# Stage A of a graph kernel: x loaded block by block into two places that TensorE reads, in place of one bulk load and a staging copy

## What is computed

```python
ones = jnp.ones((src.shape[0],), feats.dtype)
deg_out = jnp.clip(jax.ops.segment_sum(ones, src, num_segments=n), 1.0)
deg_in = jnp.clip(jax.ops.segment_sum(ones, dst, num_segments=n), 1.0)
h = feats * jax.lax.rsqrt(deg_out)[:, None]
m = jax.ops.segment_sum(h[src], dst, num_segments=n) * jax.lax.rsqrt(deg_in)[:, None]
gc = m @ W_gc + b_gc
x = gc + (feats @ W_res + b_res)
core = _moe_ff(x, Wg, bg, w1, b1, w2, b2)      # top-2 of 64 experts, gelu between two matmuls
y = x + core                                    # then batch norm over nodes, + feats, layer norm
```

## Time and profile before

| | |
|---|---|
| median of 3 runs | 1657.07 us |
| lowest, highest | 1651.96, 1659.29 us |
| the profiled execution | 1655.46 us |
| its span in the profile | 1653.6 us |
| mean granted clock of TensorE | 0.957 of full |
| TensorE matmuls busy | 1483.0 us, 90% |
| TensorE weight loads busy | 1253.0 us, 76% |
| VectorE busy | 1096.2 us, 66% |
| ScalarE busy | 697.4 us, 42% |
| GpSimd busy | 469.6 us, 28% |
| DMA on SyncE's and ScalarE's main queue | 150.59 MB, 27.8% of 16 engines' span |
| largest lines on the chain that ended last | TensorE L1070 32%, L1176 13%, L1185 12%, L1058 9%, L974 4% |

### The profile page before, as it was taken

How to read it: one execution, slowest core, us unless ns; L and a number is a source line. 1 busy time by engine, 2 the same in 40 slices (tenths; PEclk the granted TensorE clock), 3 DMA queues, 4 the chain that set the end, 5 groups by cost and what they waited for, 6 DMA issues and landing times.

```text
span 1653.6 us, 42138 instructions
## 1 busy us (share of the span) xinstructions
PE 1483.0 (90%) x11682; PEld 1253.0 (76%) x11683; DVE 1096.2 (66%) x2604; ACT 697.4 (42%) x1610; POOL 469.6 (28%) x442
## 2 busy tenths in 40 slices
PE   5988858999999999999999997699999999999662
PEld 4866747877777787777777786688888888888562
DVE  6976898787788788788778775344444444444377
ACT  1647765443434344434443442233333333333257
POOL 4356100112112112111111212455555555555100
PEclk9998979999999999999999998799999999999785
DMA  9212110101101101101101022786667856763594
GB/s 295 80 61 60 58 37 10 43 14 39 51 13 38 51 13 38 51 13 38 37 27 38 20 71 71 230 271 224 214 218 247 270 178 226 251 215 97 186 301 151
DMA packets 146095, 188.11 MB, mean 114 GB/s; under 512 B 16117, under 2 KB 114200, under 8 KB 145763
## 3 DMA queue, kind: packets, MB, share of 16 engines
q1 hardware_dynamic: 126034, 150.59, 27.8%
q0 software_dynamic: 18144, 35.99, 6.8%
q10 hardware_dynamic: 1872, 1.02, 0.2%
HBM read 141.42 MB, written 51.21 MB: 116 GB/s over the span
## 4 chain that ended last, share of the span: by engine, by line
PE 76%; DVE 6%; issue 5%; ACT 4%; DMA 2%; another core or an unknown queue 2%; DVEq 2%; SPq 1%; POOL 0%; ACTq 0%; POOLq 0%
PE banks L1070 32%; PE banks L1176 13%; PE banks L1185 12%; PE banks L1058 9%; PE banks L974 4%; DVE work L1282 3%; PE banks L955 2%; PE banks L1162 1%; ACT counts_r L803 1%; PE banks L1089 1%; DMA big<-ytab 1%; SPq L571 1%; DVE stats L1738 1%; PE banks L1079 1%
## 5 line engine op out<-in xcount | busy, mean ns | idle before, releaser
L1070 PE MATMUL banks<-parts_r,counts_r 128*128 128x512 f32 x2401 | 609.0, 401 | 13.6 <-ACT counts_r L803 12.6
L1070 PEld LDWEIGHTS banks<-parts_r,counts_r 128*128 128x128 f32 x2401 | 437.1, 189 | 107.2 <-issue 22.3
L803 ACT CAST counts_r<-banks 128x784 fp32r<-128x784 f32 x392 | 301.8, 816 | 445.1 <-PE banks L1058 426.4
L1282 DVE TENSOR_TENSOR work<-edge,iota_two 128x1024 bf16<-128x1024 bf16 (+1 forms) x784 | 435.9, 622 | 47.5 <-PE banks L1058 36.0
L637 POOL DMA_INDIRECT lists<-entry,slot x98 | 120.1, 1225 | 735.4 <-DVEq L1541 661.3
L1176 PE MATMUL banks<-work 128*128 128x128 f32 x1984 | 250.9, 280 | 11.7 <-ACT work L862 4.1
L1176 PEld LDWEIGHTS banks<-work 128*128 128x128 f32 x1984 | 233.6, 193 | 25.2 <-issue 17.0
L1185 PE MATMUL banks<-big,work 128*128 x992 | 234.7, 380 | 1.5 <-ACT work L873 1.5
L1652 DVE COPY work<-work 128x1024 f32 x125 | 94.7, 757 | 184.9 <-PE banks L1176 101.3
L1058 PEld LDWEIGHTS banks<-work 128*128 128x128 bf16 x3136 | 152.8, 98 | 71.8 <-issue 70.4
L1058 PE MATMUL banks<-work 128*128 128x98 bf16 x3136 | 184.8, 210 | 17.8 <-DVE work L1282 9.0
(11 more groups left out here) (219 smaller groups left out, 1182.6 us busy)
## 6 DMA issues: line engine op xcount, KB each, us to landing
work<-in_L_gnn_w_dram SPq DMA_DIRECT2D x64, 512.0 KB
big<-in_L_gnn_w_dram SPq DMA_DIRECT2D x64, 512.0 KB
ytab<-zeros SPq DMA_DIRECT2D x11, 1024.0 KB
big<-in_L_gnn_b_dram SPq DMA_DIRECT2D x64, 128.0 KB
restab<-big SPq DMA_DIRECT2D x7, 896.0 KB, 4.0
big<-xtab SPq DMA_DIRECT2D x7, 896.0 KB
res_mem<-restab SPq DMA_DIRECT2D x24, 256.0 KB, 2.9
xtab<-pair_mem SPq DMA_DIRECT2D x24, 256.0 KB, 2.2
```

The source lines that it names most:

```text
L803: nc.scalar.copy(counts[h][:, :, i * WB * WN:(i + 1) * WB * WN].rearrange("p b (h w) -> p h b w", h=2), built_ps[i % 2][:, :, 0:WB * WV // ...
L1070: last = pe.matmul(agg_ps[h], counts[h][:, b, :], parts[:, b, :], start=(b == 0), stop=(b == NB - 1))
L1282: return dve.tensor_tensor(hot, digits.rearrange("p (c t) -> p c t", t=2).unsqueeze(2).to_broadcast([P, c, n, 2]), iota_two[:, 0:n, :].uns ...
```

## The change

x is no longer loaded in bulk. `pair_mem[:, 0:2D]`, of which `fblk` was the first half, becomes two places `feats[0]` and `feats[1]`, and each block of x is loaded into the place of its parity by a DMA of its own (128 KB) on SyncE's queue. TensorE transposes straight out of the place and waits for its DMA (`feats_in[s]`). ScalarE's `stage_feats`, 49 copies, is gone, with its semaphore `f_staged`. Blocks 0 and 1 are loaded where the first 6 blocks were. The load of block b waits until TensorE has turned block b-2 (`fT_summed`). The seven stores to `restab` are written between the loads on the same queue, store j behind the load of block 7j+10. The 22 rows behind the end of the last block are filled by a small DMA of zeros, and the clearing of the whole block in `G` by VectorE (L1249) is gone.

```diff
+        feats = [pair_mem[:, s * D:(s + 1) * D] for s in range(2)]
+        fblk = feats[0]
...
             pad_ends(0, dst, dst_flat)
-            sp.dma_start(G[:, 0:FIRST, D:2 * D], blocks(x, 0, FIRST)).then_inc(feats_first, 16)
+            for b in range(2):
+                sp.dma_start(feats[b], x[b * P:(b + 1) * P, :]).then_inc(feats_in[b], 16)
             pad_ends(1, src, src_flat)
-            sp.dma_start(G[:, FIRST:NB - 1, D:2 * D], blocks(x, FIRST, NB - 1 - FIRST)).then_inc(feats_in, 16)
-            sp.dma_start(G[0:TAIL, NB - 1, D:2 * D], x[(NB - 1) * P:N, :]).then_inc(feats_in, 16)
             sp.wait_ge(lists_set, 1)
...
-            for j in range(NPC):
+            def store_res(j):
                 sp.wait_ge(prod_copied, (j + 1) * BLK7 + 2)
                 sp.dma_start(blocks(restab, j * BLK7, BLK7), G[:, j * BLK7:(j + 1) * BLK7, D:2 * D]).then_inc(res_out[j // LATE], 16)
+
+            for b in range(2, NB):
+                rows = P if b < NB - 1 else TAIL
+                sp.wait_ge(fT_summed, b - 1)
+                sp.dma_start(feats[b % 2][0:rows, :], x[b * P:b * P + rows, :]).then_inc(feats_in[b % 2], 16)
+                if b == NB - 1:
+                    sp.wait_ge(consts, 1)
+                    sp.dma_start(feats[b % 2][TAIL:P, :], zeros[TAIL:P, :]).then_inc(feats_in[b % 2], 16)
+                if b > BLK7 and (b - 3) % BLK7 == 0:
+                    store_res((b - 3) // BLK7 - 1)
+            store_res(NPC - 1)
...
-            def stage_feats(b):
-
-                if not isinstance(b, int) or b > 0:
-                    act.wait_ge(fT_summed, b)
-                nc.scalar.copy(fblk, G[:, ds(b, 1), D:2 * D].rearrange("p b d -> p (b d)")).then_inc(f_staged, 1)
-
...
-                if not isinstance(b, int) or b + 2 < NB:
-                    stage_feats(b + 2)
...
-            act.wait_ge(feats_first, 16)
-            stage_feats(0)
             turn_feats(0, 0)
-            stage_feats(1)
-            for b in range(FIRST - 2):
+            for b in range(2):
                 feats_step(b, b % 2)
-            act.wait_ge(feats_in, 32)
-            with act.Fori(FIRST // 2 - 1, B_FOUND[0] // 2) as i:
+            with act.Fori(1, B_FOUND[0] // 2) as i:
...
-            def turn_feats(b):
+            def turn_feats(b, s, loaded):
...
-                pe.wait_ge(f_staged, b + 1)
+                pe.wait_ge(feats_in[s], loaded)
                 for k in range(K):
-                    m = pe.transpose(fT_ps[:, k, :], fblk[:, k * P:(k + 1) * P], ident[:, :])
+                    m = pe.transpose(fT_ps[:, k, :], feats[s][:, k * P:(k + 1) * P], ident[:, :])
...
-            dve.memset(G[:, NB - 1, D:2 * D], 0.0).then_inc(tails_set, 1)
```

More of the change, by code:

```diff
@@ L59, in gnn_kernel @@
     LEAD = 3
-    FIRST = 6
     NROW = -(-E // ROW)
@@ L250, in gnn_kernel @@
         pair_x = [pair_mem[:, s * 2 * D:(s + 1) * 2 * D].rearrange("p (b d) -> p b d", b=2) for s in range(2)]
-        fblk = pair_mem[:, 0:D]
+        feats = [pair_mem[:, s * D:(s + 1) * D] for s in range(2)]
+        fblk = feats[0]
         bias_x = pair_mem[:, 2 * D:4 * D].rearrange("p (m d) -> p m d", m=2)
@@ L318, in gnn_kernel @@
         z_ps = [banks[:, 4 * s:4 * s + 4, :].rearrange("p a (b d) -> p (a b) d", d=D) for s in range(2)]
-        src_in, feats_first, feats_in, weights_in, bases_in, pads_out = sem("src_in"), sem("feats_first"), sem("feats_in"), sem("weights_in"), sem("bases_in"), [sem("dst_out"), sem("src_out")]
+        src_in, feats_in, weights_in, bases_in, pads_out = sem("src_in"), [sem("feats_in0"), sem("feats_in1")], sem("weights_in"), sem("bases_in"), [sem("dst_out"), sem("src_out")]
         tails_set, lists_set, lists_out, y_zeroed = sem("tails_set"), sem("lists_set"), sem("lists_out"), sem("y_zeroed")
@@ L326, in gnn_kernel @@
         deg_clipped, deg_root, rs_ready = sem("deg_clipped"), sem("deg_root"), sem("rs_ready")
-        f_staged, fT_summed, fT_ready = sem("f_staged"), sem("fT_summed"), sem("fT_ready")
+        fT_summed, fT_ready = sem("fT_summed"), sem("fT_ready")
         multiplied, prod_copied = sem("multiplied"), sem("prod_copied")
@@ L975, in multiply, with feats_total, feats_step @@
                 last.then_inc(multiplied, 1)
-            def feats_step(b, s, pair=None):
-                if not isinstance(b, int) or b + 1 < NB:
-                    turn_feats(b + 1)
+            def feats_total(b):
+                return 16 * (b // 2 + 1) + (16 if b == NB - 1 else 0)
+            def feats_step(b, s, pair=None, i=None):
+                if i is not None:
+                    turn_feats(b + 1, 1 - s, i * 16 + 16 * (s + 1))
+                elif b + 1 < NB:
+                    turn_feats(b + 1, 1 - s, feats_total(b + 1))
                 if pair is not None:
@@ L1009, in _ @@
             pe.wait_ge(weights_in, NW)
-            turn_feats(0)
+            turn_feats(0, 0, feats_total(0))
             with pe.Fori(0, (G_DIGITS - LEAD) // 2) as i:
                 for s in range(2):
-                    feats_step(i * 2 + s, s, i * 2 + (s + LEAD))
+                    feats_step(i * 2 + s, s, i * 2 + (s + LEAD), i)
             for b in range(G_DIGITS - LEAD, B_DIGITS):
@@ L1247, in _ @@
             dve.memset(padends[:, 0, :], NOWHERE)
-            dve.memset(padends[:, 1, :], N)
-            dve.memset(G[:, NB - 1, D:2 * D], 0.0).then_inc(tails_set, 1)
+            dve.memset(padends[:, 1, :], N).then_inc(tails_set, 1)
             dve.memset(zeros[:, :], 0.0)
```

## The result

| | before | after |
|---|---|---|
| median | 1654.51 us (4 runs, 1648.03 to 1659.29) | 1725.06 us (4 runs, 1721.48 to 1729.42) |
| profiled execution, span | 1655.46, 1653.6 us | 1721.48, 1719.9 us |
| mean granted clock of TensorE | 0.957 | 0.945 |

The ratio is 1.0429, with a 95% interval of 1.0399 to 1.0458: 70 us slower, where 1656.0 us was forecast in a range of 1647 to 1664.

A forecast was written before the change was run, and what follows sets the result against it. It took stage A as mostly bound by TensorE and VectorE, with ScalarE setting the end only in 176:190. Terms of -0.3, -1.1 and +0.3 gave -1.1 us, median 1657.07 to 1656.0 us, range 1647 to 1664.

The forecast's parts named there:

- the later stages as long as they were: Sign that the forecast was right: the stages behind stage A keep their length; no size given.
- Rival 2: Stage A: loads of x come late behind stores or beside the gathers, TensorE idles; 17 us, 1674 us; chance 0.11.
- The sum: All terms for stage A together: -0.3 - 1.1 + 0.3 = -1.1 us.
- Bulk load gone: First DMA burst ends some 18 us sooner without x's bulk load, but nobody waits for it: gain 0.
- Start: TensorE's second turn no longer waits for the staging copy, only for ScalarE emptying the PSUM tile: gain 0.3 us.
- 176 to 190 us: Stretch of stage A with ScalarE nearly full: TensorE's turn at 190.77 no longer waits for a staging copy, gain 1.1 us.
- 94 to 176 us: Window steps of stage A: no ScalarE on the chain, so dropping its staging copies gains 0; ceiling 7.0 us.
- The first rival: ScalarE carries the window steps, so all 18 steps' copies come back: 8.8 us in all, 1648 or 1644 us; chance 0.21.
- Loads: 49 added 128 KB loads on SyncE's queue, 2.7 us each, hidden in 5.7 or 3.5 us: cost 0.
- the store ahead of a load: Plain steps: block 46's load queues behind a 896 KB store on SyncE; loss 0.3 us, bounds 0 to 1.5.
- Nothing moves: Rival: changed timing meets the same stalls elsewhere and the 1.1 us goes with them; 1657 us, chance 0.20.
- The 0.2 us for the semaphore: Allowance added to each load's 2.5 us landing, and to the load behind a store, before TensorE can use it.

The follow-up runs named there:

- The six fast forms: Changed kernel with 23, 46, 68 or 174 idle increments at ScalarE's start, 46 ahead of its expert loop, or 46 plus 20 per turn: ratios 0.9985 to 0.9997.
- the run with the loop at 650: Changed kernel plus 46 idle semaphore increments at ScalarE's start, putting its expert loop back at instruction 650: 1632.39 us, ratio 0.9985.
- the displaced kernel before with 212 increments: Kernel before, none of the change, plus 212 idle semaphore increments at ScalarE's start, expert loop at instruction 861: 1708.73 us, ratio 1.0450.
- the two displaced kernels of before: Kernel before plus 212 or 84 idle increments at ScalarE's start, expert loop at 861 or 733: 1708.73 and 1712.16 us, ratios 1.0450 and 1.0487.
- the kernel with 68 increments: Changed kernel plus 68 idle semaphore increments at ScalarE's start, expert loop at instruction 672: ratio 0.9994.

## Why the prediction was wrong

The step that failed is one that the prediction wrote down without a price: "the later stages as long as they were". It took the stages behind stage A for untouched, since no line of theirs is changed, and its sum has no term for them. But the edit moves 45 instructions out of ScalarE's code, and with them the place of a loop that runs some 800 us later. Of the 66.3 us between the two profiled executions 64.9 lie there, and they go when the loop is put back. None of the rivals had this mechanism either. Rival 2 was on the right side for the wrong reason: no turn waited for a load.

The Trainium skill, "Runtime: NRT & Kernel Launch", section "Instruction fetch mechanics", would have been the warning: it says that a taken branch whose target lies outside the window of two blocks forces a fetch, a stall. The runs agree with that. They don't agree with its sizes for ScalarE, blocks of 16 KiB or 256 instructions with two held: packets were of 8.2 KB, and a loop of 316 instructions was slow at places 128 apart, four of the eight tried, which such blocks don't allow. The section calls the cost of crossing a block's boundary mostly hidden; for the way back to the head of this loop it was 65 us in 16 turns.

The terms themselves can be read off the kernels whose loop is in a fast place, where the change is alone but for the increments.
- **The sum**, -1.1 us. The six fast forms of the changed kernel gave ratios of 0.9985, 0.9997, 0.9994, 0.9995, 0.9991 and 0.9991, 0.9992 on average, which is -1.3 us. Each interval reaches to 1, so no single run shows the sign. Together they do: on the three chips the fast forms are on average 2.3, 0.9 and 1.6 us faster than before, weighted by their scatter 1.2 us with a standard error of 0.4. Part of that can be the increments' doing (see the start). The one fast form without any at ScalarE's start, with 46 ahead of the expert loop, is 0.6 us faster on average, which is within its scatter.
- **Bulk load gone**, 0. As forecast: the DMA share of 0:50 falls from 0.80 to 0.49, and nobody gains by it.
- **Start**, -0.3. The turn that had waited 1.79 us for the staging copy waits in the run with the loop at 650 for the other copy only:

```profile
29.52 0.67 PE L966 MATMUL banks<-ident,pair_mem 128*128 128x128 f32 x2
...
30.97 0.68 PE L966 MATMUL banks<-ident,pair_mem 128*128 128x128 f32 x2 [0.78 <-ACT xTp L712]
```

The wait is now released by the copy that the prediction had named as next, L705 of before. It is shorter by 1.0 us, not 0.3, because that copy too starts sooner behind the first turn, 0.94 us instead of 1.73. But that comes with the increments: in the changed kernels that have some at ScalarE's start the copy starts 0.70 to 0.94 us behind, in those that have none 1.56 to 1.73, as in before. Why stays open. In after:

```profile
29.18 0.67 PE L963 MATMUL banks<-ident,pair_mem 128*128 128x128 f32 x2
...
31.41 0.68 PE L963 MATMUL banks<-ident,pair_mem 128*128 128x128 f32 x2 [1.57 <-ACT xTp L709]
```

From turn to turn it is 2.23 us here and 31.35 - 28.89 = 2.46 in before, so the change itself gave 0.2. The term was right in its cause and near in its size.
- **176 to 190 us**, -1.1. The same run, against the wait of 1.06 at 190.77 in the earlier trace rows:

```profile
187.40 0.41 PE L966 MATMUL banks<-ident,pair_mem 128*128 128x128 f32 x2
187.64 1.89 PE L975 MATMUL banks<-res_mem,xTp 128*128 128x256 f32 x8
189.51 0.41 PE L966 MATMUL banks<-ident,pair_mem 128*128 128x128 f32 x2
```

From turn to turn it is 189.51 - 187.40 = 2.11 us. In the displaced kernel before with 212 increments, on the same chip, it is 190.96 - 187.76 = 3.20, with the wait of 1.06 us for the staging copy. 1.09 us gained. In after the same two turns are at 192.19 and 194.17, 1.98 us apart. In the run with the loop at 650 the chain of this stretch, where ScalarE's window counts were 41.1%, names no line of ScalarE among those of 1.4% and more.
- **94 to 176 us**, 0 with a ceiling of 7.4. ScalarE saves its 5 to 6 us there and TensorE does no more for it: 761 matmuls in 94:176 in the run with the loop at 650, 761 and 758 in the two displaced kernels of before on the same chip, though its clock there was lower, 0.90 against 0.96 and 0.94. The whole of stage A settles it: on that chip stage B begins 1.0 to 3.0 us sooner in the two changed kernels than in the two of before, not 8.8. The first rival, ScalarE carrying the window steps, falls.
- **Loads**, 0, and **the store ahead of a load**, +0.3. Hidden. In the plain steps of after a store is issued at 196.93 and the load behind it, of block 46, at 198.48. Block 46 is turned at 201.96, and the turns around it are 1.95 us apart with no wait among them:

```profile
198.07 0.38 PE L963 MATMUL banks<-ident,pair_mem 128*128 128x128 f32 x2
...
200.01 0.38 PE L963 MATMUL banks<-ident,pair_mem 128*128 128x128 f32 x2
...
201.96 0.38 PE L963 MATMUL banks<-ident,pair_mem 128*128 128x128 f32 x2
```

TensorE's 98 turn matmuls have no wait that names a DMA in the whole trace. Four short ones, 2.6 us in all, name nothing; before had three, of 1.9. So the 0.3 for the load behind the store was 0, the overlapping end of its bounds. The stores land in 4.2 us where they took 4.0. The traces give no landing time for the small loads themselves, so the 2.5 us is bounded from above only: less than the 3.5 us of two plain steps. The 0.2 us for the semaphore in both terms was taken from no row, and no run shows it; since the loads were hidden with it, it decided nothing.
- **Nothing moves**, the third rival, holds as far as any one comparison can tell.

Stage B began 4.2 us later in after than in before (251.9 against 247.7) and was level with it by its end (1021.6 against 1020.9). I don't count this as an effect of the change. In the two kernels on one chip whose only difference is a few increments ahead of ScalarE's expert loop or at its start and in it, stage B began at 247.6 and 243.1 us, so single profiles differ by as much. On the chip of the first four runs the changed form began it at 246.9 and 245.4, the form before at 247.9 and 248.4.

## What to carry to other kernels

An edit that takes instructions out of an engine moves every loop behind them in that engine's code, and on ScalarE a loop that reaches into a fourth piece of 128 instructions was fetched anew in each turn. Ask this of each loop that follows an edit, and look at the packets of the instruction queue and at waits that end in "issue" once per turn. If they are there, displace the loop with idle instructions before judging the edit: here 23 to 68 of them turned 4% slower into no measurable difference. Not any number will do: with 117 it was still 3% slower.

## What the runs showed of the hardware

- ScalarE's code is fetched in packets of 8.2 KB (the packets that came and went with the place of its loop), and the cost goes by pieces of 128 instructions: a loop of 316 is fast at starts 627, 650, 672 and 778 of its code and slow at 605, 721, 733 and 861. A loop that touched three pieces brought 25 or 26 packets in the whole run, one that touched four 102 to 104, some 4.8 a turn. How many pieces are kept, and in which order they are replaced, isn't shown; nor whether the other engines have the same limit.
- In after the stand of ScalarE that holds a turn's refetch was mostly 5 to 12 us, some 2 of them usual, and TensorE had 3.8 us of waiting in each turn with 1 us of slower multiplies behind it (15.9 / 16).
- Idle instructions are cheap where an engine has time: 20 more in each turn cost nothing measurable.
- The same kernel differs by chip: 1607.4 us on one, 1634.65 and 1635.2 on two others, and 1654.51 in the runs of the main comparison. On the first of these, TensorE had a granted clock of 1.00 in 94:176 and made 924 matmuls there in the kernel with 68 increments; on another, with 46, it had 0.90 and made 761. Stage B began at 225.6 us on the one and at 246.9 on the other. The waits of stage A whose releaser is unknown ("remote": 18 us on ScalarE and VectorE in 94:176 in before, 20 with 46 increments) don't occur there at all on the first chip; what they are stays open.
